# Four attention layers on one core: row-group maxima, value matmuls in two halves of 256 queries, key loads on another queue

## The chip, the cores and the metric

The kernel runs on one core of one Trainium2 chip. The metric is the device time of one execution in microseconds (us). Lower is better.

## What is computed

The program is a stack of four transformer layers on 2048 tokens of width 256. Each layer is `x + cross_attention(layernorm(x), context)` followed by `x + mixture_of_experts(layernorm(x))`. The context has 1601 rows of width 192. Layers 0, 1 and 3 have 16 heads of width 16, layer 2 has 8 heads of width 32. Cut to what the change touches:

```python
q = (x @ Wq + bq).reshape(B, Sq, H, D).transpose(0, 2, 1, 3)      # 2048 queries
k = (y @ wk + bk).reshape(B, -1, H, D).transpose(0, 2, 1, 3)      # 1601 keys
v = (y @ wv + bv).reshape(B, -1, H, D).transpose(0, 2, 1, 3)
attn = jax.nn.softmax(q @ k.swapaxes(-1, -2) / sqrt(D), axis=-1)
x = x + (attn @ v).transpose(0, 2, 1, 3).reshape(B, Sq, E) @ wo + bo
```

## The kernel before

**Tiling.** The queries are cut into 4 blocks of 512, the heads into 4 groups (four heads of width 16, or two of width 32), the keys into 13 tiles of 128 (the last has 65). For each block and each group, 13 steps run over the key tiles. So a layer has 208 steps. The first and the last block are written out, the two in the middle are a hardware loop.

**Precision by stacking.** Queries and keys are split into three bf16 parts each. The tile `k_stack` (`KS`) holds parts of the keys in its partitions, `q_stack` (`QS`) the matching parts of the queries, so that one bf16 matmul over the partitions adds up six products of parts. For heads of width 16 the six products take 96 partitions. Partition 96 holds the mask (or zero) against ones. Partitions 97 to 99 hold ones against the three parts of the negated row maximum. Heads of width 32 need two such stacks (`nsub` is 2), added in the accumulator.

**The work of a step.** `scores` (L1863) multiplies 128 keys by 512 queries, one matmul per head and stack, four in a step. It takes 100 partitions, so the maximum is already subtracted. ScalarE turns each pair of accumulator banks into probabilities (L986). `weigh` (L1877) multiplies the probabilities of the step before by the values `V`: four heads of 32 columns each, one beside the other in the partitions of bank 4, in float32, which makes two passes for each. They are 4 matmuls of 512 queries in the program and 8 in the trace (layer 2: 2 heads of 64 columns, 4 in the trace).

**The side jobs.** The row maxima of a later group are computed ahead, as side jobs that are spread over the steps by `side_schedule` (L66). A "max" job is a matmul of 128 queries by 400 keys over 97 partitions (L1826; two matmuls, over 97 and 96 partitions, in layer 2), into one of three banks in turn, and a maximum over its 400 columns by VectorE (L1257). A bank is reused after VectorE has read it (the wait `sf.at(2)`). Most steps have five such jobs (layer 2: two or three). Other side jobs are "turn" (transposes the maxima, L1829), "den" and "spread" (the denominators, L1832 and L1836), "out" (the output projection, L1848), "turn_x" and "query" (the queries of the next block, L1841 and L1763). In each step two side jobs stand ahead of the scores, the rest between them, and the value matmuls stand at the end. Ahead of the steps, `side_prologue` computes all maxima of group 0 and some of group 1.

**Queues.** SyncE (the queue SP) issues nearly all DMAs in program order: `load_queries` (L474, L480), `store_max_rows` (L489, L494), `store_key_parts` (L437) and `load_keys` (L461). During the experts of layers 0 and 2, `next_keys` stores the key parts of the next layer in eight pieces and, after the fourth and the eighth, waits until they have landed and issues 12 key loads. ScalarE copies each projected piece (L922, L923) into one of two buffers, which come free when their store has landed; GpSimd (POOL) splits it.

Of the kernel before, what the change touches and what calls it, by code (L numbers as in the profile page):

```python
# [6 lines left out]
P = 128  # L7
NT = T // P
Q = 512
# [26 lines left out]

class Count:
# [27 lines left out]

def side_schedule(g, hpg, first, last):  # L66
# [11 lines left out]
    late = [("max", (g + 1) % NG, u, c) for u in range(half, units) for c in range(4)] if nxt1 else []  # L78
    early = [("max", (g + 2) % NG, u, c) for u in range(half) for c in range(4)] if nxt2 else []
# [19 lines left out]
def max_jobs(g, hpg, lo, hi):  # L99
    return [("max", g, u, c) for u in range(lo, hi) for c in range(4)]  # L100
# [35 lines left out]
def build(nc, A, out):  # L136
# [13 lines left out]
    with ctx:  # L150
# [46 lines left out]
        with att:  # L197
# [5 lines left out]
            KS = sb("k_stack", [100, 16, S], bf16, att)  # L203
            V = sb("v", [P, NK, 512], f32, att)
            QS = [sb(f"q_stack{i}", [100, 4, Q], bf16, att) for i in range(4)]
# [9 lines left out]
        with ln2:  # L215
            sb("skip_sums", [P, 4 * 2 * Q + 2 * Q + 16 + Q + NG * Q], f32, ln2)
            sb("skip_keys", [100, 16, S], bf16, ln2)
            sb("skip_values", [P, NK, 512], f32, ln2)
            XN = sb("xn", [P, NT, D], f32, ln2)
# [100 lines left out]
        s_ks = [sem(f"s_ks{g}") for g in range(NG)]  # L320
        s_ql = [sem(f"s_ql{i}") for i in range(4)]
# [59 lines left out]


        @block.sync
        def _(sp):
# [34 lines left out]
            def load_constant_rows(L):  # L419

                ones_flat = const_rows[0:1, 0:S]
                rows = [(96, mask_row if L == 3 else zero_row)]
                if L in (0, 2):
                    rows += [(97, ones_flat), (98, ones_flat), (99, ones_flat)]
                for row, src in rows:
                    sp.dma_start(KS[row:row + 1, :, :], src.unsqueeze(1).to_broadcast([1, 16, S]))\
                      .then_inc(s_ksc, 16)
# [26 lines left out]
            def load_keys(L, g):  # L454

                dh, nsub, hpg = ATT[L]["dh"], ATT[L]["nsub"], ATT[L]["hpg"]
                for row in range(6):
                    part = [0, 1, 2, 0, 1, 0][row]
                    src = k_parts[part].rearrange("(h d) s -> d h s", d=dh)[:, g * hpg:(g + 1) * hpg, :]
                    r, sub = (row, 0) if nsub == 1 else (row % 3, row // 3)  # L460
                    sp.dma_start(KS[r * dh:(r + 1) * dh, 4 * g + sub:4 * g + 4:nsub, :], src)\  # L461
                      .then_inc(s_ks[g], 16)

            def load_queries(L, t, buf):
# [5 lines left out]
                dst = QS[buf]  # L470
                if a["nsub"] == 1:
                    for row, part in enumerate([0, 0, 0, 1, 1, 2]):
                        src = q_parts[part].rearrange("(h d) t -> d h t", d=dh)[:, g * hpg:(g + 1) * hpg, cols]
                        sp.dma_start(dst[row * dh:(row + 1) * dh, :, :], src).then_inc(s_ql[buf], 16)  # L474
                else:
                    for row, part in enumerate([0, 0, 0, 1, 1, 2]):
                        src = q_parts[part].rearrange("(h d) t -> d h t", d=dh)[:, g * hpg:(g + 1) * hpg, cols]
                        r = row % 3
                        sp.dma_start(dst[r * dh:(r + 1) * dh, row // 3::2, :], src).then_inc(s_ql[buf], 16)
                sp.dma_start(dst[96:97, :, :], ones_row).then_inc(s_ql[buf], 16)  # L480

            def store_max_rows(L, g):
# [11 lines left out]
                sp.dma_start(QS[g][96:100, 0:4:a["nsub"], :], src).then_inc(s_mr, 16)  # L494
# [25 lines left out]
            load_keys(0, 0)  # L520
            load_keys(0, 1)

            for L in range(4):
# [8 lines left out]
                if L == 0:  # L532
# [3 lines left out]
                    load_keys(0, 2)  # L536
                    load_keys(0, 3)
# [61 lines left out]
                def next_keys():  # L599

                    if L in (0, 2):
                        load_constant_rows(L + 1)
# [21 lines left out]
                elif L == 1:  # L624
# [39 lines left out]
                    for g in range(NG):  # L664
                        load_keys(2, g)
# [57 lines left out]
        def _(pool):  # L723
# [69 lines left out]
            for L in range(4):  # L793
# [887 lines left out]
        def _(pe):  # L1681
# [4 lines left out]
            ksc, ks, ql, mr = Count(s_ksc), [Count(s) for s in s_ks], [Count(s) for s in s_ql], Count(s_mr)  # L1686
# [65 lines left out]
            for L in range(4):  # L1752
# [21 lines left out]
                ksc.step({0: 4 * 16, 1: 16, 2: 4 * 16, 3: 16}[L])  # L1774
                pe.wait_ge(s_ksc, ksc.at())
                for g in range(NG):
                    ks[g].step(6 * 16)
                for q in range(3):
                    ql[q].step(7 * 16)
                njob, pair, used, turned = [0], [0], [0], [0]  # L1780
                sel = sel16 if dh == 16 else sel32
# [4 lines left out]
                def side(job):  # L1786
# [3 lines left out]
                    if job[0] == "max":  # L1790
                        _, g, u, c = job
                        if u == 0 and c == 0:
                            pe.wait_ge(s_ql[g], ql[g].at())
                            pe.wait_ge(s_ks[g], ks[g].at())
# [470 lines left out]
```

## Time and profile before

| | before |
|---|---|
| median of 3 runs | 4478.63 us (4469.84 to 4485.76) |
| profiled execution | 4481.04 us |
| its span, first to last instruction | 4479.3 us |
| mean granted TensorE clock | 0.926 |
| TensorE matmul busy | 4004.6 us, 89% |
| VectorE busy | 2650.2 us, 59% |
| ScalarE busy | 1937.9 us, 43% |
| GpSimd busy | 322.4 us, 7% |

The page of the profile gives the busy time of each engine over the whole span. The four attention stages lie at about 116 to 775, 1223 to 1885, 2473 to 3104 and 3403 to 4066 us, with the experts between them. PE is TensorE's matmuls, PEld its weight loads. A matmul's duration in the trace has the fill and the drain of the array in it, so the distance from one start to the next is the better measure of what a matmul costs.

### The profile page before, as it was taken

Reading aid. Unit: us, or ns where it says so; the run is one execution under the profiler, and the core shown is the slowest. Engines: PE = TensorE matmul, PEld = TensorE weight load, DVE = VectorE, ACT = ScalarE, POOL = GpSimd, SP = SyncE. Lnnn points to the kernel's source line nnn. Section 1 sums busy time; section 2 is a strip of 40 time slices with the busy share of each in tenths; the row PEclk is TensorE's granted clock in tenths of the full one; section 3 lists DMA queues with packets and bytes.
Section 4 is the critical chain, followed back from the end, with each engine's and each line's share of the span. In section 5 each row is a group of like instructions: output and inputs, shape, how many; then the busy total and the mean of one; then the engine's idle time right before and its main releaser. Section 6 shows DMA issues by size and latency. Waiting matters only on the chain. (4 is left out here: it accounts for less than half of the span.)

```text
span 4479.3 us, 60914 instructions
## 1 busy us (share of the span) xinstructions
PE 4004.6 (89%) x19174; PEld 1813.1 (40%) x19175; DVE 2650.2 (59%) x5801; ACT 1937.9 (43%) x2306; POOL 322.4 (7%) x588
## 2 busy tenths in 40 slices
PE   5999999799899999948993999998889999996894
PEld 2333333566333333335662343443532333333563
DVE  5888785445788888532224555443258887874122
ACT  1567667222166766712331334333103666763110
POOL 2100000200010000040002100000101000000202
PEclk8999999799699999958996999999697999997997
DMA  6000000400000000052104000000400000001145
GB/s 126 25 16 13 13 9 2 82 19 19 24 26 16 10 13 9 1 198 95 32 29 104 26 15 12 12 8 19 66 20 27 20 11 13 10 4 67 61 143 106
DMA packets 131861, 170.58 MB, mean 38 GB/s; under 512 B 30840, under 2 KB 111936, under 8 KB 129539
## 3 DMA queue, kind: packets, MB, share of 16 engines
q1 hardware_dynamic: 121986, 136.07, 11.7%
q0 software_dynamic: 9600, 31.04, 2.4%
q8 instruction: 149, 2.44, 0.2%
q14 instruction: 126, 1.02, 0.1%
HBM read 114.12 MB, written 54.66 MB: 38 GB/s over the span
## 5 line engine op out<-in xcount | busy, mean ns | idle before, releaser
L1257 DVE TENSOR_REDUCE mx<-ps 128x1 f32<-128x400 f32 (+1 forms) x3584 | 1809.0, 565 | 491.1 <-PE ps L1826 482.5
L986 ACT ACTIVATE probs<-ps,zero_col 128x1024 f32<-128x1024 f32 (+1 forms) x1040 | 1113.3, 1111 | 889.5 <-PE ps L1863 889.4
L1826 PE MATMUL ps<-k_stack,q_stack 97*128 97x400 bf16 (+3 forms) x4096 | 1219.5, 347 | 74.5 <-issue 34.8
L1863 PE MATMUL ps<-q_stack,k_stack 100*128 100x512 bf16 (+2 forms) x3328 | 1081.6, 382 | 4.0 <-ACT probs L986 4.0
L1877 PE MATMUL ps<-probs,v 128*32 128x512 f32 (+2 forms) x5824 | 891.9, 607 | 0.2 <-ACT probs L986 0.2
L1826 PEld LDWEIGHTS ps<-k_stack,q_stack 97*128 97x128 bf16 (+1 forms) x4096 | 343.9, 98 | 1173.7 <-DVE mx L1257 712.3
L986 ACT ACTIVATE probs<-ps,mask_col 128x1024 f32<-128x1024 f32 (+1 forms) x416 | 441.0, 1110 | 259.6 <-PE ps L1863 259.6
L1863 PEld LDWEIGHTS ps<-q_stack,k_stack 100*128 100x128 bf16 (+2 forms) x3328 | 324.7, 100 | 315.7 <-ACT probs L986 55.8
L1532 DVE SCALAR_TENSOR_TENSOR x_res<-ps,comb,x_res 128x256 f32<-128x256 f32 x336 | 148.3, 482 | 175.7 <-PE ps L2027 168.6
L1877 PEld LDWEIGHTS ps<-probs,v 128*32 128x32 f32 (+2 forms) x5824 | 140.0, 111 | 228.4 <-issue 220.2
L2027 PE MATMUL ps<-w_down_s,h_t_s 128*128 128x256 f32 x640 | 149.5, 381 | 4.3 <-ACT h_t_s L1088 4.1
L2091 PE MATMUL ps<-w_all,xn_t 128*128 x624 | 144.6, 385 | 3.8 <-ACT xn_t L1056 2.4
L2012 PE MATMUL ps<-xn_t,w_up_s 128*128 128x512 f32 x320 | 147.2, 592 | 0.8 <-issue 0.8
L2070 PE MATMUL ps<-w_all,xn_t 128*128 x312 | 142.7, 600 | 0.4 <-issue 0.4
L2027 PEld LDWEIGHTS ps<-w_down_s,h_t_s 128*128 128x128 f32 x640 | 120.6, 190 | 50.7 <-issue 35.5
L1848 PE MATMUL ps<-wo,o_t 128*128 128x256 f32 x512 | 130.7, 405 | 11.0 <-DVE mx L1257 7.6
L2091 PEld LDWEIGHTS ps<-w_all,xn_t 128*128 128x128 f32 x624 | 118.1, 192 | 43.0 <-issue 28.4
L1056 ACT ACTIVATE xn_t<-ps,tile_bias 128x128 f32<-128x128 f32 x312 | 84.7, 383 | 99.6 <-PE ps L2082 99.4
L1088 ACT ACTIVATE h_t_s<-ps 128x512 f32<-128x512 f32 x80 | 46.7, 596 | 177.0 <-PE ps L2012 176.9
L740 POOL MEMSET wv<- 1x256 f32 x4 | 1.2, 304 | 1670.6 <-DVEq L376 1670.3
L1848 PEld LDWEIGHTS ps<-wo,o_t 128*128 128x128 f32 x512 | 99.3, 200 | 40.7 <-DVE mx L1257 20.5
L2045 PE MATMUL ps<-w_up_s,xn_t 128*128 128x512 f32 x256 | 112.2, 601 | 0.8 <-DVE x_res L1499 0.8
(250 smaller groups left out, 2823.9 us busy)
## 6 DMA issues: line engine op xcount, KB each, us to landing
q_stack<-q_parts SPq DMA_DIRECT2D x384, 64.0 KB, 2.2
k_stack<-k_parts SPq DMA_DIRECT2D x96, 200.1 KB
q_parts<-qk_part SPq DMA_DIRECT2D x32, 384.0 KB, 2.5
w_up<-in_up SPq DMA_DIRECT2D x17, 704.0 KB, 4.3
x_place<-zeros POOLq DMA_DIRECT2D x2, 5120.0 KB, 28.6
k_parts<-qk_part SPq DMA_DIRECT2D x24, 384.0 KB, 3.2
w_all<-in_up SPq DMA_DIRECT2D x5, 1024.0 KB, 21.4
w_all<-in_down SPq DMA_DIRECT2D x5, 1024.0 KB, 23.6
```

The lines of the kernel that those rows point to most:

```text
L986: act.activation(PR[pair[0] % 4][0:r, :, :], PS[0:r, 2 * b:2 * b + 2, :], ACT.Exp, bias=mask_col[0:r, k:k + 1] if L == 3 else zero_col[0:r ...
L1257: ins = dve.reduce_max(MX4[g % 2][:, u, c:c + 1], PS[:, bank, 0:CK[c]], AX.X)
L1532: dve.scalar_tensor_tensor(X[:, t, :], PS[:, b, 0:D], c, X[:, t, :], ALU.mult, ALU.add).then_inc(s_yf, 1)
L1826: last = mm(PS[:, bank, 0:CK[c]], QS[g][0:rows, s, qt * P:(qt + 1) * P], KS[0:rows, ks0, CKO[c]:CKO[c] + CK[c]], start=sub == 0, stop=sub ...
L1848: last = mm(PS[:, bank, 0:D], OT[:, g, i * P:(i + 1) * P], WO[:, g, :], start=g == 0, stop=g == NG - 1)
L1863: last = mm(PS[0:r, b + i, :], KS[0:rows, (g * hpg + jj) * nsub + sub, k * P:k * P + r], QS[g][0:rows, slot_of(jj) + sub, :], start=sub == ...
L1877: last = mm(PS[pw * jj:pw * jj + pw, 4, :], V[0:r, k, (g * hpg + jj) * pw:(g * hpg + jj) * pw + pw], PR[used[0] % 4][0:r, i, :], start=k = ...
L2012: last = mm(PS[0:rows, b, :], up[:, k, off + at:off + at + rows], xnT[:, k, c * Q:(c + 1) * Q], start=k == 0, stop=k == 1)
L2027: last = mm(PS[:, b, 0:D], HTF[(c - 1) % 2][0:rows, t, i * P:(i + 1) * P], WDF[par][0:rows, t, :], start=t == 0, stop=t == len(ft) - 1)
L2045: last = mm(PS[:, t % 8, :], xnT[:, k, t * P:(t + 1) * P], WUS[par][:, k * 512:(k + 1) * 512], start=k == 0, stop=k == 1)
L2070: last = mm(PS[:, half, :], XT1[par][:, k * P:(k + 1) * P], w1.rearrange("p a f -> p (a f)"), start=k == 0, stop=k == 1)
L2091: last = mm(PS[:, 4 + par, 0:D], HB[:, q * P:(q + 1) * P], w2.rearrange("p a f -> p (a f)"), start=q == 0, stop=q == NF // P - 1)
```

## The change

1. **Rows.** For heads of width 16, even heads keep their most significant products (k0q0, k1q0, k0q1) in partitions 0 to 47 and the mask in 48; odd heads keep them in 64 to 111 and the mask in 112, with the other products in the partitions that are left. The odd heads get a seventh product. `scores` then takes 100 partitions for even heads and 116 for odd ones.
2. **Maxima.** A max job takes 49 partitions only (0 to 48, or 64 to 112), and `max_order` lets even and odd heads alternate. In layer 2 it takes the first stack alone: one matmul instead of two.
3. **Value matmuls in halves.** `weigh` runs all heads of queries 0 to 255, then up to two side jobs (`between`), then all heads of queries 256 to 511. `places` sets where side jobs stand: in a step of five, two ahead of the scores, one in their middle, two between the halves.
4. **Loads.** Keys of heads of width 16 take 13 DMAs for a group instead of 6, queries 15 instead of 7, the rows of maxima 2 instead of 1.
5. **Queue.** The key loads for layers 1 and 3 are issued by GpSimd, after all eight pieces are split and their stores have landed, and no longer by SyncE in the middle of the stores.

```diff
+ROWS = ([(0, 0, 0), (16, 1, 0), (32, 0, 1), (52, 2, 0), (68, 1, 1), (84, 0, 2)],
+        [(64, 0, 0), (80, 1, 0), (96, 0, 1), (0, 2, 0), (16, 1, 1), (32, 0, 2), (48, 2, 1)])
+MROW, MAX_ROWS, ALL_ROWS = (48, 112), ((0, 49), (64, 113)), (100, 116)
+def max_order(hpg):
+    if hpg == 2:
+        return [(u, c) for u in range(2 * TPQ) for c in range(4)]
+    return [((2 * j + odd) * TPQ + t, c) for j in range(2) for t in range(TPQ) for c in range(4) for odd in range(2)]
+def places(n, npair):
+    if npair == 1:
+        return [min(n, 1), max(n - 1, 0) // 2, 0, max(n - 1, 0) - max(n - 1, 0) // 2]
+    between, ahead = min(n, 2), min(max(n - 2, 0), 2)
+    rest = n - ahead - between
+    mid = (rest + 2) // 3
+    return [ahead, (rest - mid + 1) // 2, mid, (rest - mid) // 2, 0, between]
@@ next_keys (SyncE)
-                        if L != 1 and u % 4 == 3:
-                            wait_landed(kd)
-                            load_keys(L + 1, u // 2 - 1)
-                            load_keys(L + 1, u // 2)
@@ GpSimd, after split_keys
+                if L in (0, 2):
+                    for c in staged.landed["key"]:
+                        pool.wait_ge(c.sem, c.at())
+                    for g in range(NG):
+                        load_keys(pool, L + 1, g)
@@ side, "max"
-                        for sub in range(nsub):
-                            rows = 97 if sub == 0 else 96
-                            s = slot_of(j) + sub
-                            ks0 = (g * hpg + j) * nsub + sub
-                            last = mm(PS[:, bank, 0:CK[c]], QS[g][0:rows, s, qt * P:(qt + 1) * P],
-                                      KS[0:rows, ks0, CKO[c]:CKO[c] + CK[c]], start=sub == 0, stop=sub == nsub - 1)
+                        lo, hi = MAX_ROWS[j % 2] if nsub == 1 else (0, 97)
+                        last = mm(PS[:, bank, 0:CK[c]], QS[g][lo:hi, slot_of(j), qt * P:(qt + 1) * P],
+                                  KS[lo:hi, (g * hpg + j) * nsub, CKO[c]:CKO[c] + CK[c]], start=True, stop=True)
@@ weigh
+                    for half in range(2):
+                        cols = slice(half * Q // 2, (half + 1) * Q // 2)
+                        for j in range(npair):
...
+                                last = mm(PS[pw * jj:pw * jj + pw, 4, cols],
+                                          V[0:r, k, (g * hpg + jj) * pw:(g * hpg + jj) * pw + pw],
+                                          PR[(used[0] + j) % 4][0:r, i, cols], start=k == 0 and half == 0, stop=k == NK - 1,
...
+                        if half == 0:
+                            for job in between:
+                                side(job)
```

## Rows read from the trace of the kernel before

**Rows 1.** The page, busy time: engine, us (share), instructions.

```profile
PE 4004.6 (89%) x19174; PEld 1813.1 (40%) x19175; DVE 2650.2 (59%) x5801; ACT 1937.9 (43%) x2306; POOL 322.4 (7%) x588
```

**Rows 2.** Busy time by stretch: stretch, length, busy of each engine, clock, DMA share, GB/s.

```profile
116.00:775.00 659.00, 646.78 (x3754) 229.08 (x3753) 521.69 (x1103) 454.10 (x445) 21.18 (x24) 1.00 0.04 13
2473.00:3104.00 631.00, 629.11 (x2928) 248.90 (x2926) 306.02 (x632) 245.69 (x237) 21.17 (x24) 1.00 0.04 13
1850.00:1884.00 34.00, 32.81 (x197) 7.46 (x194) 5.56 (x16) 31.78 (x32) 0.00 (x0) 1.00 0.01 1
2452.00:2471.00 19.00, 16.57 (x71) 4.11 (x69) 18.39 (x42) 0.00 (x0) 0.00 (x0) 1.00 0.14 41
```

**Rows 3.** Timeline of PE, layer 0: start us, us, work, count.

```profile
402.05 1.07 PE L1877 MATMUL ps<-probs,v 128*32 128x512 f32 x8
403.05 0.52 PE L1826 MATMUL ps<-k_stack,q_stack 97*128 97x401 bf16 x2
403.41 0.59 PE L1863 MATMUL ps<-q_stack,k_stack 100*128 100x512 bf16 x2
403.84 0.33 PE L1826 MATMUL ps<-k_stack,q_stack 97*128 97x400 bf16 x1
404.01 0.38 PE L1863 MATMUL ps<-q_stack,k_stack 100*128 100x512 bf16 x1
...
404.62 0.33 PE L1826 MATMUL ps<-k_stack,q_stack 97*128 97x401 bf16 x1
404.89 1.06 PE L1877 MATMUL ps<-probs,v 128*32 128x512 f32 x8
```

**Rows 4.** The same at the end of layer 1, steps without side jobs.

```profile
1849.95 1.04 PE L1863 MATMUL ps<-q_stack,k_stack 100*128 100x512 bf16 x4
1850.92 1.06 PE L1877 MATMUL ps<-probs,v 128*32 128x512 f32 x8
1851.91 0.60 PE L1863 MATMUL ps<-q_stack,k_stack 100*128 100x512 bf16 x2
```

**Rows 5.** Timeline of PE, experts of layer 3: transposes of 128 and 64 partitions.

```profile
4255.45 0.38 PE L2153 MATMUL ps<-ident,x_expert 128*128 128x128 f32 x2
4255.77 0.27 PE L2153 MATMUL ps<-ident,x_expert 64*128 64x64 f32 x1
4255.97 0.44 PE L2153 MATMUL ps<-ident,x_expert 128*128 128x128 f32 x2
```

**Rows 6.** Timeline of DVE, the maxima of one step of layer 0.

```profile
403.43 2.50 DVE L1257 TENSOR_REDUCE mx<-ps 128x1 f32<-128x401 f32 x5
```

**Rows 7.** Timeline of PE, layer 2, one step with three max jobs.

```profile
2906.87 1.08 PE L1877 MATMUL ps<-probs,v 128*64 128x512 f32 x4
2907.88 0.86 PE L1826 MATMUL ps<-k_stack,q_stack 97*128 97x401 bf16 x4
2908.58 1.03 PE L1863 MATMUL ps<-q_stack,k_stack 100*128 100x512 bf16 x4
2909.55 1.08 PE L1877 MATMUL ps<-probs,v 128*64 128x512 f32 x4
```

**Rows 8.** Timelines of SP and PE, the start of layer 1's maxima.

```profile
1172.42 2.69 SPq L474 DMA_DIRECT2D q_stack<-q_parts  x6
1175.16 0.53 SPq L480 DMA_DIRECT2D q_stack<-const_rows  x1
1177.29 3.22 PE L1826 MATMUL ps<-k_stack,q_stack 97*128 97x401 bf16 x7 [8.33 <-issue]
```

**Rows 9.** Timelines of SP, ACT, DVE, PE and landing of stores, experts of layer 0.

```profile
835.86 7.03 SPq L461 DMA_DIRECT2D k_stack<-k_parts  x12
859.78 0.60 ACT L922 ACTIVATE qk<-ps 128x512 f32<-128x512 f32 x1 [22.23 <-DMA k_parts<-qk_part]
848.04 0.42 DVE L1431 TENSOR_TENSOR comb<-prob_s,r_s 128x256 f32<-128x256 f32 x1
869.66 0.69 PE L2012 MATMUL ps<-xn_t,w_up_s 128*128 128x512 f32 x1 [0.82 <-issue]
DMA to landing us min/median/max: 16.7/17.0/17.2
```

**Rows 10.** Timeline of ACT, experts of layer 2, the same wait.

```profile
3196.15 0.60 ACT L922 ACTIVATE qk<-ps 128x512 f32<-128x512 f32 x1 [19.80 <-DMA k_parts<-qk_part]
```

**Rows 11.** GpSimd's DMA issues of L853, ns min/median/max.

```profile
L853 POOL DMA_DIRECT2D w_all<-in_up x3: 543/561/592, 2027.0 to 2029.2; - x3
```

More of the change, by code:

```diff
@@ L77, in side_schedule @@
     half = units * 3 // 8
-    late = [("max", (g + 1) % NG, u, c) for u in range(half, units) for c in range(4)] if nxt1 else []
-    early = [("max", (g + 2) % NG, u, c) for u in range(half) for c in range(4)] if nxt2 else []
+    late = max_jobs((g + 1) % NG, hpg, half, units) if nxt1 else []
+    early = max_jobs((g + 2) % NG, hpg, 0, half) if nxt2 else []
     jobs = late + early[:6] + ([("turn", (g + 1) % NG)] if nxt1 else []) + early[6:]
@@ L320, in build @@
         s_ks = [sem(f"s_ks{g}") for g in range(NG)]
+        s_kt = [sem(f"s_kt{g}") for g in range(NG)]
         s_ql = [sem(f"s_ql{i}") for i in range(4)]
@@ L380, in key_rows, with load_keys @@
             return P if k < NK - 1 else KREM
+        def load_keys(eng, L, g):
+            dh, nsub, hpg = ATT[L]["dh"], ATT[L]["nsub"], ATT[L]["hpg"]
+            done = s_kt[g] if L in (1, 3) else s_ks[g]
+            heads = k_parts.rearrange("r (h d) s -> r d h s", d=dh)[:, :, g * hpg:(g + 1) * hpg, :]
+            if nsub == 1:
+                for odd in range(2):
+                    for row, part, _ in ROWS[odd]:
+                        eng.dma_start(KS[row:row + dh, 4 * g + odd:4 * g + 4:2, :], heads[part][:, odd::2, :])\
+                           .then_inc(done, 16)
+            else:
+                for i, (_, part, _) in enumerate(ROWS[0]):
+                    sub, r = i // 3, i % 3 * dh
+                    eng.dma_start(KS[r:r + dh, 4 * g + sub:4 * g + 4:2, :], heads[part]).then_inc(done, 16)
         @block.sync
@@ L421, in load_constant_rows @@
                 ones_flat = const_rows[0:1, 0:S]
[L422 to L427, printed above, removed]
+                rows = [mask_row if L == 3 else zero_row] + [ones_flat] * 3
+                for i, src in enumerate(rows):
+                    if ATT[L]["nsub"] == 1:
+                        for odd in range(2):
+                            sp.dma_start(KS[MROW[odd] + i:MROW[odd] + i + 1, odd::2, :],
+                                         src.unsqueeze(1).to_broadcast([1, 8, S])).then_inc(s_ksc, 16)
+                    else:
+                        sp.dma_start(KS[96 + i:97 + i, 0::2, :], src.unsqueeze(1).to_broadcast([1, 8, S]))\
+                          .then_inc(s_ksc, 16)
             def store_key_parts(u):
@@ L493, in store_max_rows @@
                 src = m_parts[:, 0:units * P].rearrange("r (j x) -> r j x", x=Q)
-                sp.dma_start(QS[g][96:100, 0:4:a["nsub"], :], src).then_inc(s_mr, 16)
+                if a["nsub"] == 1:
+                    for odd in range(2):
+                        sp.dma_start(QS[g][MROW[odd]:MROW[odd] + 4, odd::2, :], src[:, odd::2, :]).then_inc(s_mr, 16)
+                else:
+                    sp.dma_start(QS[g][96:100, 0::2, :], src).then_inc(s_mr, 16)
             x_chunks = A["x"].rearrange("(c t p) d -> c p t d", t=TPQ, p=P)
@@ L1918, in iteration @@
                                     pe.wait_ge(s_os, cs.at())
-                                weigh(g, k - 1)
+                                weigh(g, k - 1, jobs)
+                            else:
+                                for job in jobs:
+                                    side(job)
                 njobs = sum(len(s) for g in range(NG) for s in side_schedule(g, hpg, False, False))
```

110 lines of the change are left out of this document (54 added, 56 removed).

## The prediction

> **What bounds the kernel now.** I read the busy times first [rows 1]: PE is busy 89% of the span. Then I read the stretches of the attention stages [rows 2]: in layer 0 PE is busy 647 of 659 us at full clock, VectorE 522, ScalarE 454. So attention, some 2614 of the 4479 us, is paced by PE in program order, with VectorE next. Then I read one step [rows 3]. From value block to value block it lasts 404.89 - 402.05 = 2.83 us, and PE never pauses: a max matmul starts its successor 0.17 us later (403.84 to 404.01), a scores matmul 0.215 us later (403.41 plus two of them is 403.84). Five maxima and four scores are 0.86 + 0.86 = 1.72 us. That leaves 1.11 us for the value block. A matmul's duration has some 0.17 us of fill and drain in it (a scores matmul lasts 0.38 and is followed after 0.215), so of the block's 1.07 us it streams 0.90, with a seam of 0.05 between its two passes: 0.85 us of columns. So about 0.25 us of each step is neither.
>
> Where these 0.25 us lie is the key to the change. The last max starts at 404.62 and is through at 404.79, yet the values start at 404.89: 0.10 us. The values end their streaming near 402.95, yet the next max starts at 403.05: 0.10 us. The other 0.05 us goes to the seam between the two passes. Steps without side jobs show the same [rows 4]: the scores start at 1849.95, four of them are through at 1850.81, the values start at 1850.92. The array pauses about 0.10 us whenever the shape of the tile changes, from 128 columns to 32 and back. A change in the number of rows costs the same: a transpose of 128 partitions is followed after 0.11 us by its like (the pair at 4255.45 lasts 0.38 us, one of them 0.27), but the one of 64 partitions starts only at 4255.77, 0.21 us after the second, and the next one of 128 partitions again 0.20 us later, though the 64 columns between them need half as long [rows 5]. I price one switch at 0.10 us, bounds 0.09 and 0.15.
>
> **The change, part by part.**
>
> *Layers 0, 1, 3: switches.* A step of five now has two switches. New order: two maxima (49 partitions), two scores, one max, two scores, first value half, two maxima, second value half. That is a switch in front of each of these seven blocks: five more, +0.50 us. A step with "den", "spread", "out" or "query" as its sixth job has ten, eight more. Walked through all 208 steps by the diff's placing, a layer gets 1095 more switches: +110 us (bounds 99 and 164).
>
> The Trainium skill says the same in TensorEngine Tiling (Array Packing), Key Properties: changing the tiling mode, not merely the tile, drains the engine. By that rule, too, five more pauses stand in a step; the trace agrees with it at 0.10 us each.
>
> *Pairs.* Two neighbouring maxima now lie in partitions 0 to 48 and 64 to 112 and go to different banks. The value matmuls show that tiles side by side in columns run together (four heads in one block of 1.07 us [rows 3], where one after the other would be four times as long). For tiles side by side in rows the trace has nothing. Bounds: the second max is free (saves 0.17 us) or costs its full 0.17 us. I take nearly free, saving 0.16, since the column case is the nearest row. A layer has 320 such pairs: -51 us.
>
> The same skill, TensorE: Matmul & The Clock Gate, Part 3, states that matmuls in distinct row groups overlap, with 3.07 times the speed for four; no run here shows it yet.
>
> *Halves.* The second half repeats the seam between passes and loads the values' weights again: 0.04 us in 207 value blocks, +8 us.
>
> *VectorE's chain.* It takes 0.48 us a maximum (five in 2.50 us, the last one 0.56) and starts 0.38 us after the matmul (403.05 to 403.43) [rows 3, 6]. With three banks, the second max ahead of the scores needs the bank of the first max between the halves: 0.38 + 0.56 + about 0.05 us after that one's start, 0.99 us. PE is there after 0.18 (pair) + 0.10 + 0.47 (half) + 0.10 = 0.85 us. So a new wait of 0.13 us stands in each of 123 steps of five, +16 us, with the scores queued behind it. Against it go waits of PE on VectorE that exist now around "out", "den" and "query" jobs, 659 - 647 = 12 us in a layer [rows 2], most of which slower steps cover: -12.
>
> Sum of a layer: 110 - 51 + 8 + 16 - 12 = +71 us (a step of five: 2.83 + 0.50 - 0.32 + 0.04 + 0.13 = 3.18). Three layers: **+213 us**.
>
> *Layer 2.* A step of two max jobs lasts 2909.55 - 2906.87 = 2.68 us, with four max matmuls from 2907.88 to 2908.58 [rows 7]; one of three jobs is two matmuls longer, 3.02. One matmul a job goes, 0.17 us each; the maxima keep 97 partitions, so they switch only around the value halves: +0.20 and +0.04. Three jobs: -0.52 + 0.24 = -0.28; two: -0.34 + 0.24 = -0.10. Over the layer's steps 468 jobs save 80 us, 382 more switches and 207 seams add 38 + 8: **-34 us** (bounds -38 and -14, by the price of a switch). VectorE is busy 306 of 631 us [rows 2] and does not take over.
>
> *Query and maxima loads.* SP needs 2.69 us for six issues, 0.45 each [rows 8]. The first maxima wait for the first buffer: eight issues more, 3.6 us, in each of layers 0, 1 and 3. In layer 0 the key loads and two further buffers stand in the same queue ahead of the rows of maxima, with 14 more issues a pair of groups; PE is at most some 10 us later there. Inside the steps a group lasts some 40 us and hides 7 us of issues; if that cover were gone each group would start up to 4 us late. Together **+18 us** (bounds 8 and 30).
>
> *Key loads.* Today the stores of pieces five and six stand behind 12 key loads and land after 17.0 us; ScalarE waits 22.23 us for the buffer (there is nothing else to put it to), and with it the values' projections, which PE needs before its experts at 869.66 [rows 9]. Without the loads ahead, such stores land in about 3 us. So 14 us come back in layer 0; VectorE's routing is done at 848.5 [rows 9], PE would start near 855, so it is late next and doesn't bind. In layer 2 the wait is 19.80 us [rows 10], some 13 us come back. **-27 us** (bounds -34 and 0). GpSimd's 52 loads, at its 0.56 us an issue [rows 11], are 29 us, and it is idle for 280 us of experts in layer 0 and 130 in layer 2: hidden.
>
> **The sum.** +213 - 34 + 18 - 27 = +170 us on the profiled 4481.0, 4651. The median of the runs shown lies 2.4 us lower: 4649, in round numbers 4650 us, 3.8% slower.
>
> **The rivals.**
>
> *Row switches are free* (chance 0.12). If going between 49 and 97 or more partitions costs nothing, and only value blocks pause, 709 of the 1095 switches of a layer go, -71 us. VectorE's chain gives part back: a step of five would be 2.68 + 0.04 + 0.13 = 2.85 us, no better than now. So a layer is at +12 us at most, at 0 if the chain runs smoother: 0 to 36 for three, with - 34 + 18 - 27 that is 4436 to 4472: not slower. It decides from a row switch under about 0.03 us. Rows 5 speak against it.
>
> *Pairs don't overlap* (0.10). Then 51 us a layer stay and the wait of 16 goes: +35 each, 4755. Against it: the value block.
>
> *49 partitions are not treated as a smaller tile* (0.08). Then the change does not do what it says: maxima run one after the other, but without row switches. A layer has 390 more switches around and between the halves: 39 + 8 - 12 = +35; total 3 x 35 - 43 = +62, 4541. Against it: the transposes of 64 partitions.
>
> *Density* (0.07). A step of five gets 50 matmuls and weight loads for 34. If the clock drops for a tenth of the steps, 2.2 us of streaming double there: 0.1 x 624 x 2.2 = 137 us, 4787; a PE that can't be fed so densely would look similar. Against a drop: at the end of layer 1, 16 steps (32 activations) take 34 us and stream 1.71 of 2.13 us each, 80%; in layer 2's prologue 71 matmuls of 0.17 us stream 12 of 19 us, 63%. Both kept clock 1.00 [rows 2]; the new step streams 2.2 of 3.18 us, 70%.
>
> **How the numbers follow.** The forecast case holds 0.63 and spans 4590 to 4710 (switch price, loads). The range takes in the second rival and the third, 4515 to 4760, 0.8 of the chance; free row switches and a drop of density stay outside. Within 0.3% (what can be told from no change here) is 4465 to 4492. Faster: 0.07, from free row switches. Same: 0.04. Slower: 0.89.
>
> **What would show it.** In the profile after: pairs of L1826 that start within 0.02 us of each other; 0.10 us between a pair's end and the next scores; steps of five near 3.18 us; in layer 2 steps of three near 2.75 us; the ACT wait on the key stores near 3 us instead of 22; PE's first expert matmul of layer 0 some 15 us sooner after the end of attention. I would be wrong if the gap at a change from 49 to 100 partitions were much smaller than 0.10 us in bf16, if the pairs were serial, or if VectorE's chain held PE longer than 0.13 us a step.

## The result, and the profile after the change

The changed kernel takes 4680.3 us (median of 4 runs, 4670.6 to 4685.0), the one before 4474.3 us (median of 4, 4469.8 to 4485.8). The ratio is 1.046, with a 95% interval of 1.044 to 1.048. The forecast was 4650 us in a range of 4515 to 4760, slower with a chance of 0.89.

| | before | after |
|---|---|---|
| profiled span | 4479.3 us | 4675.1 us |
| mean granted clock | 0.926 | 0.915 |
| first scores of layer 0 | 116.2 us | 145.0 us |
| scores stage, layer 0 | 658.8 us | 728.0 us |
| layer 1 | 661.2 us | 734.7 us |
| layer 2 | 630.7 us | 610.7 us |
| layer 3 | 663.0 us | 740.0 us |
| step of five max jobs (median start to start) | 2.83 us | 3.205 us |

The page of the changed kernel first, busy times of its engines (engine, us, share):

```profile
PE 4244.2 (91%) x24486; PEld 1833.5 (39%) x24487; DVE 2684.1 (57%) x5801; ACT 1943.1 (42%) x2306; POOL 374.2 (8%) x692
```

PE issues 5312 matmuls more than in [rows 1] (5824 more in the value blocks, which are cut in two, 512 fewer maxima in layer 2) and stays the engine that paces. The four attention stages, read by stretch (stretch, length, busy PE, PEld, DVE, ACT, POOL, clock, DMA share, GB/s), against [rows 2]:

```profile
145.00:873.00 728.00, 720.93 (x5402) 235.79 (x5401) 527.95 (x1103) 454.75 (x445) 21.21 (x24) 0.99 0.05 12
1315.00:2050.00 735.00, 728.24 (x5402) 236.92 (x5403) 528.94 (x1104) 455.07 (x444) 21.21 (x24) 0.98 0.05 12
2637.00:3247.00 610.00, 608.29 (x3284) 243.52 (x3283) 319.77 (x634) 247.26 (x237) 21.20 (x24) 0.98 0.04 13
3535.00:4275.00 740.00, 732.87 (x5401) 236.96 (x5399) 528.73 (x1104) 454.99 (x444) 21.20 (x24) 0.97 0.05 12
```

VectorE's and ScalarE's times in layer 0 are those of before within 1.3%. PE's work was rearranged, and the stage is 69 us longer. One step of layer 0, the timeline of PE (start us, us, work, count), which answers [rows 3]:

```profile
402.55 0.64 PE L1922 MATMUL ps<-probs,v 128*32 128x256 f32 x8
403.12 0.51 PE L1868 MATMUL ps<-k_stack,q_stack 49*128 49x400 bf16 x2
403.56 0.61 PE L1905 MATMUL ps<-q_stack,k_stack 100*128 100x512 bf16 x2
404.10 0.34 PE L1868 MATMUL ps<-k_stack,q_stack 49*128 49x400 bf16 x1
404.37 0.61 PE L1905 MATMUL ps<-q_stack,k_stack 100*128 100x512 bf16 x2
404.91 0.64 PE L1922 MATMUL ps<-probs,v 128*32 128x256 f32 x8
405.48 0.34 PE L1868 MATMUL ps<-k_stack,q_stack 49*128 49x400 bf16 x2
405.76 0.62 PE L1922 MATMUL ps<-probs,v 128*32 128x256 f32 x5
```

Read the starts. The single max of 404.10 is followed by scores at 404.37, after 0.27 us; before it was 0.17 [rows 3]. Two scores from 403.56 would be through at 403.99, and the max starts at 404.10. Each change of shape costs 0.10 us, also between 49 and 100 partitions. The pair at 405.48 lasts 0.34 us in all, as long as one: its two matmuls start at 405.483 and 405.486. The pair at 403.12 lasts 0.51 us: the second starts 0.165 us after the first, when VectorE has freed its bank. VectorE's line for the step, against [rows 6]:

```profile
402.65 2.50 DVE L1298 TENSOR_REDUCE mx<-ps 128x1 f32<-128x400 f32 x5 [0.66 <-PE ps L1868]
```

It takes the same 2.50 us for five maxima, and it had waited 0.66 us for PE before them.

A step of three jobs in layer 2, against [rows 7]:

```profile
2905.59 0.65 PE L1922 MATMUL ps<-probs,v 128*64 128x256 f32 x4
2906.17 0.34 PE L1868 MATMUL ps<-k_stack,q_stack 97*128 97x401 bf16 x1
2906.44 0.65 PE L1922 MATMUL ps<-probs,v 128*64 128x256 f32 x4
2907.03 0.34 PE L1868 MATMUL ps<-k_stack,q_stack 97*128 97x400 bf16 x1
2907.21 0.60 PE L1905 MATMUL ps<-q_stack,k_stack 100*65 100x512 bf16 x2
2907.65 0.33 PE L1868 MATMUL ps<-k_stack,q_stack 97*128 97x400 bf16 x1
2907.82 0.60 PE L1905 MATMUL ps<-q_stack,k_stack 100*65 100x512 bf16 x2
2908.35 0.65 PE L1922 MATMUL ps<-probs,v 128*64 128x256 f32 x4
```

It lasts 2908.35 - 2905.59 = 2.76 us. The maxima of 97 partitions sit beside the scores without a pause (2907.03 to 2907.21, 0.18), and pay 0.10 us only at the value halves.

### The profile page after: what moved, and what is told of

The parts are those of the page before. It is cut to its first block and busy times, and to the rows that moved or that the text cites. A ratio compares the mean times of both kernels' runs of the same rounds, so it can differ in the third digit from the quotient of the medians.

```text
span 4675.1 us, 72302 instructions
## 1 busy us (share of the span) xinstructions
PE 4244.2 (91%) x24486; PEld 1833.5 (39%) x24487; DVE 2684.1 (57%) x5801; ACT 1943.1 (42%) x2306; POOL 374.2 (8%) x692
## 5 line engine op out<-in xcount | busy, mean ns | idle before, releaser
L1298 DVE TENSOR_REDUCE mx<-ps 128x1 f32<-128x400 f32 (+1 forms) x3584 | 1840.3, 567 | 668.2 <-PE ps L1868 660.2
L1868 PE MATMUL ps<-k_stack,q_stack 49*128 49x400 bf16 (+3 forms) x3584 | 1002.4, 359 | 77.7 <-issue 41.5
L1922 PE MATMUL ps<-probs,v 128*32 128x256 f32 (+2 forms) x11648 | 1071.7, 397 | 1.1 <-ACT probs L1027 1.1
L1905 PE MATMUL ps<-q_stack,k_stack 100*128 100x512 bf16 (+4 forms) x3328 | 1029.3, 390 | 6.1 <-ACT probs L1027 6.1
L1868 PEld LDWEIGHTS ps<-k_stack,q_stack 49*128 49x128 bf16 (+1 forms) x3584 | 281.6, 94 | 1109.6 <-DVE mx L1298 603.7
L1922 PEld LDWEIGHTS ps<-probs,v 128*32 128x32 f32 (+2 forms) x11648 | 287.1, 112 | 507.2 <-issue 483.8
L1905 PEld LDWEIGHTS ps<-q_stack,k_stack 100*128 100x128 bf16 (+4 forms) x3328 | 246.5, 100 | 344.7 <-issue 244.6
```

Of the source, the lines that this page charges most:

```text
L1298: ins = dve.reduce_max(MX4[g % 2][:, u, c:c + 1], PS[:, bank, 0:CK[c]], AX.X)
L1868: last = mm(PS[:, bank, 0:CK[c]], QS[g][lo:hi, slot_of(j), qt * P:(qt + 1) * P], KS[lo:hi, (g * hpg + j) * nsub, CKO[c]:CKO[c] + CK[c]], s ...
L1905: last = mm(PS[0:r, b + i, :], KS[0:rows, (g * hpg + jj) * nsub + sub, k * P:k * P + r], QS[g][0:rows, slot_of(jj) + sub, :], start=sub == ...
L1922: last = mm(PS[pw * jj:pw * jj + pw, 4, cols], V[0:r, k, (g * hpg + jj) * pw:(g * hpg + jj) * pw + pw], PR[(used[0] + j) % 4][0:r, i, cols ...
```

## The experiments

All edits start from the kernel before or from the changed one, as said. Ratios are to the kernel before, on the same chip, with 95% intervals. "Step of five" is the median distance between the first value matmuls of steps with five max jobs.

**1. The halves alone.** The kernel before with the value blocks in halves and the new places; its maxima keep 97 partitions.

```diff
+                    for half in range(2):
+                        cols = slice(half * Q // 2, (half + 1) * Q // 2)
...
+                        if half == 0:
+                            for job in between:
+                                side(job)
```

> The kernel before with the value matmuls in halves and the new places of the side jobs alone; maxima keep 97 partitions, loads and queues stay. Theory (a change of tile shape costs 0.10 us, either in rows or columns): only the halves add switches, two in a step, +0.20 +0.04, so a step of five side jobs goes from 2.83 to about 3.07 us, layers 0, 1 and 3 grow by 30 to 45 us each (to 690 to 705), layer 2 by 45 (to 676), in all 4610 to 4650 us. Rival (the halves themselves, their reloads and the dense stream of instructions cost the time, and the rows of the maxima cost nothing): a step of five is at 3.2 us or more here too, as it is in the changed kernel with its 3.205. Start of layer 0's steps: if its delay of 29 us in the changed kernel comes from the clock under 49-partition maxima, it is back at about 116 us here.

4617.1 us, ratio 1.034 (1.031 to 1.037). Step of five 3.073 us, layers 0, 1 and 3 at 692.8, 692.7 and 693.9 us. That is two switches and a seam on 2.83 us: 0.20 + 0.04. So the halves by themselves cost 3.4%. This isn't a share of the 4.6%, for experiment 3 has no halves and loses 3.9%. Splitting a block that is alone in its shape adds two switches when a job of another shape stands in the cut.

**2. Neighbouring maxima in the same 64 partitions.** The changed kernel with another order, so that no two neighbours lie in different row groups.

```diff
-    return [((2 * j + odd) * TPQ + t, c) for j in range(2) for t in range(TPQ) for c in range(4) for odd in range(2)]
+    return [(u, c) for u in range(4 * TPQ) for c in range(4)]
```

> The changed kernel, but neighbouring max jobs belong to the same head, so both lie in the same 64 partitions and can't run side by side. Theory (pairs in different partitions really overlap, 0.16 us each): the pair between the value halves takes 0.33 instead of 0.17 us, while the pair ahead of the scores is already 0.165 us apart for VectorE's bank; a step of five goes from 3.205 to about 3.37 us, a layer by +25 to +35 us, all three +75 to +105, total 4755 to 4785. Rival (the overlap is only in the records, the array shares its time): no change beyond 0.3%, 4680.

4806.6 us, ratio 1.076 (1.065 to 1.087), step of five 3.379 us, 0.174 more than with the pairs. Timeline of PE, layer 0:

```profile
404.27 0.64 PE L1922 MATMUL ps<-probs,v 128*32 128x256 f32 x8
404.84 0.51 PE L1868 MATMUL ps<-k_stack,q_stack 49*128 49x401 bf16 x2
405.29 0.64 PE L1922 MATMUL ps<-probs,v 128*32 128x256 f32 x8
```

The two maxima between the halves take 0.51 us instead of 0.34. Of the two pairs of a step, 0.16 each, one is given back as the wait for VectorE's bank. So the rival "pairs don't overlap" is out: the pairs work, but they earn less than the row switches that they need. The total lies above the 4755 to 4785 us that were expected, and the clock has part in it: in the middle of layers 0, 1 and 3 it stood at half for 48, 31 and 44 us, in the changed kernel for 7, 24 and 17.

**3. Whole value blocks, maxima at their old places.**

```diff
-                    for half in range(2):
-                        cols = slice(half * Q // 2, (half + 1) * Q // 2)
+                    for j in range(npair):
```

> The changed kernel with its value matmuls whole and the side jobs placed as in the kernel before (two ahead, the rest one by one between the scores); rows, maxima and loads as changed. Theory (0.10 us for each change between 49 and 100 or 116 partitions): a step of five has eight switches, six more than before, and one pair, so about 3.26 us although no value matmul is split; layers 0, 1, 3 at 730 to 745 us; layer 2, with one matmul a job and no halves, at about 553 us, a three-job step at 2.50; total 4610 to 4640. Rival (halves are the cost): a step of five at or under 2.83 us, layers at 660 or less, total near 4400.

4640.1 us, ratio 1.039 (1.036 to 1.042), step of five 3.276 us, though no value block is split. The old places put maxima between the scores one by one, which makes six row switches: 2.83 + 6 x 0.10 - 0.16 for the one pair = 3.27.

**4. Whole value blocks, maxima in two clusters.** Two ahead of the scores, the rest together behind them.

```diff
                                     scores(g, k, j, i)
-                                    for job in slot[cut[2 * j + i]:cut[2 * j + i + 1]]:
-                                        side(job)
+                            for job in slot[2:]:
+                                side(job)
```

> The changed kernel with whole value matmuls and the side jobs in two groups, two ahead of the scores and all others behind them, ahead of the values. Theory: a step of five has four switches (into and out of the values, out of and into the maxima), two more than before, and two pairs side by side: 1.965 + 3 x 0.172 + 0.20 + some 0.05 of waiting for VectorE = 2.74 us against 2.83 before; layers 0, 1, 3 at 660 to 668, layer 2 at 553, total 4400 to 4440, under the kernel before by 1 to 2 percent. Rival (VectorE is the bound once maxima come in threes): steps of five at 2.9 us or more, total over 4470.

4455.0 us, ratio 0.9965 (0.9951 to 0.998), above the 4400 to 4440 us that was expected. The step came out: 2.759 us.

```profile
402.29 0.34 PE L1868 MATMUL ps<-k_stack,q_stack 49*128 49x400 bf16 x2
402.57 1.04 PE L1905 MATMUL ps<-q_stack,k_stack 100*128 100x512 bf16 x4
403.55 0.58 PE L1868 MATMUL ps<-k_stack,q_stack 49*128 49x400 bf16 x3
404.05 1.06 PE L1919 MATMUL ps<-probs,v 128*32 128x512 f32 x8
```

Two added switches (+0.20) against 0.27 that pairs save. Yet layer 0 takes 681.4 us, 23 more than before. One reason is the other steps: with all jobs in one cluster PE waits for VectorE's banks, as its list of waits in layer 0 says (who, for what: us, times, longest).

```profile
PE ps L1890 <- DVE mx L1298: 6.8, 12, 0.9
PE ps L1874 <- DVE mx L1298: 6.1, 13, 0.5
PE ps L1878 <- DVE mx L1298: 6.0, 13, 0.5
```

Before, the waits for VectorE in layer 0 were 6.6 us in all. The 43 steps with five max jobs and "den", "spread" or "out" take 0.29 us more each, 12 us. The larger reason is the clock: in layer 0 it stands at half for 39.0 us in all, in seven stretches, and for 3.7 us before. At half of each stretch that is some 18 us (an estimate), while the 123 steps of five give back 9. The gain of the total is layer 2's (552.3 us).

**5. A shorter VectorE chain.** The changed kernel with each maximum over half of its columns; the other half of the maxima's keys is left out.

```diff
-dve.reduce_max(MX4[g % 2][:, u, c:c + 1], PS[:, bank, 0:CK[c]], AX.X)
+dve.reduce_max(MX4[g % 2][:, u, c:c + 1], PS[:, bank, 0:CK[c] // 2], AX.X)
```

> The changed kernel, but VectorE takes each maximum over 200 of the 400 columns (it leaves out half of each row of scores in the maxima, so the subtracted value is not always the largest). Theory (VectorE's turn on the three banks holds the second max ahead of the scores 0.165 us behind the first in every step of five): the reduction falls from 0.56 to about 0.35 us, the two maxima ahead start within 0.01 us, a step of five goes from 3.205 to 3.04 us, a layer by 20 to 22 us, total 4610 to 4625. Rival (the second max waits for the array, not for its bank): no change of the 0.165 us, total 4680.

4576.2 us, ratio 1.020 (1.017 to 1.023). The step of five is 3.043 us, as expected, 0.16 less than 3.205. So VectorE holds PE 0.16 us in a step of five and no more: with maxima of 0.37 us instead of 0.57 the kernel is still 2.0% slower than before. The total is lower than expected because the maxima ahead of the steps also became shorter, by 14 us in layers 1 and 3, 8 in layer 2 and 7 in layer 0, which the expectation had missed.

**6. More loads.** The kernel before with the keys' and queries' loads cut by even and odd heads, 12 and 13 DMAs a group for 6 and 7.

```diff
-                        sp.dma_start(dst[row * dh:(row + 1) * dh, :, :], src).then_inc(s_ql[buf], 16)
+                        for odd in range(2):
+                            sp.dma_start(dst[row * dh:(row + 1) * dh, odd::2, :], src[:, odd::2, :]).then_inc(s_ql[buf], 16)
```

> The kernel before with its key and query loads of layers 0, 1 and 3 cut by odd and even heads: 24 instead of 12 key loads for two groups, 13 instead of 7 query loads, the same bytes; maxima with 97 partitions as before. It asks why the steps of layer 0 begin at 145 us in the changed kernel and at 116 before. Theory (under 49-partition maxima the granted clock of the prologue stays at the lower level, so its projections take twice as long): the loads alone cost 4 to 8 us, scores begin at 120 to 124 us. Rival (the longer queue of SyncE delays the rows of maxima): scores begin at 140 us or later. Layers 1 and 3: first maxima 2.7 us later. Total +10 to +16 us, or +35 by the rival.

4491.8 us, ratio 1.001 (1.000 to 1.003), 6 us more where 10 to 16 were expected; first scores at 123.2 us. The loads cost 2 to 7 us of the 29 at the start: with the loads of before the first scores come at 116.2 us in the kernel before and at 119.0 to 120.9 in experiments 1, 7, 8 and 9.

**7. The queue of the key loads.** The kernel before; GpSimd issues the key loads of layers 1 and 3 behind its splits.

```diff
-                        if L != 1 and u % 4 == 3:
-                            wait_landed(kd)
-                            load_keys(L + 1, u // 2 - 1)
-                            load_keys(L + 1, u // 2)
+                    for g in range(NG):
+                        load_keys(pool, L + 1, g)
```

> The kernel before with part 5 of the change alone: the 24 key loads of layers 1 and 3 are issued by GpSimd after all stores have landed. Theory (the stores of pieces five and six no longer queue behind the loads): ScalarE's wait of 22 us in the experts of layer 0 falls to 3 to 5, PE begins those experts 14 to 17 us sooner, in layer 2 13 to 15 us, total -27 to -32 us, 4436 to 4441 against 4467. Rival (the loads now compete with the experts' weights and give it back): PE waits for weights in the experts of layer 0, the gain under 15 us.

4457.9 us, ratio 0.993 (0.991 to 0.995). From the last scores to the first expert matmul it is 77.8 us in layer 0 (94.7 before) and 102.2 in layer 2 (118). Part of it is lost again: the experts of layer 0 take 11 us more. PE waits 9.07 us there for weights, which SyncE loads beside the keys. PE's timeline, and from the list of DMAs GpSimd's loads (count, KB each, median us to landing):

```profile
897.72 2.07 PE L2017 MATMUL ps<-xn_t,w_up_s 128*128 128x512 f32 x2 [9.07 <-DMA w_down_s<-in_down]
...
k_stack<-k_parts POOLq DMA_DIRECT2D x24, 200.1 KB, 16.2
```

**8. One maximum matmul in layer 2.** The kernel before; in layer 2 the products of the second stack are left out of the maxima, as in the changed kernel.

```diff
-                        for sub in range(nsub):
+                        last = mm(PS[:, bank, 0:CK[c]], QS[g][0:97, slot_of(j), qt * P:(qt + 1) * P],
```

> The kernel before with one matmul instead of two in each max job of layer 2 (97 partitions, the products of the first stack; the maximum is then of slightly coarser scores, which softmax allows), values whole, places as before. Theory: PE is the bound of layer 2, so each job gives 0.17 us: steps of three jobs 3.02 to 2.50 us, of two 2.68 to 2.33, 468 jobs 80 us, layer 2 from 631 to about 552 us, total 4386 to 4390 against 4467. Rival (VectorE or ScalarE takes over): steps of three stay over 2.7 us, the gain under 50 us.

4406.3 us, ratio 0.982 (0.980 to 0.984). Layer 2 takes 551.9 us. In the changed kernel it takes 610.7: 59 of the 79 us that this part alone earns are given back. Some 50 of them are the halves', the rest is a stretch of 20.5 us at half clock.

**9. The two good parts together.** Experiments 7 and 8 in one kernel.

> The kernel before with two parts of the change alone, each measured by itself already: GpSimd issues the key loads of layers 1 and 3 after all stores have landed (0.993 of before), and layer 2's maxima take one matmul over the first stack instead of two (0.982; as in the changed kernel, the products of the second stack are left out of the maxima). Rows, order and places of layers 0, 1 and 3 stay as before, so no switch of tile shape is added. My theory: the two parts act in different stages and add up, 0.993 x 0.982 = 0.975 of before, about 4370 us, between 4360 and 4390; layer 2's attention stage 552 us, last scores to first expert matmul 78 us in layer 0 and 102 in layer 2, the experts of layer 0 about 289 us. Rival: the sooner start of the experts is worth something only when layer 2 ends as before; now that layer 2's steps are paced more tightly, the two overlap in what they save, and the sum is near that of the larger part alone, 4400 us or more.

4369.8 us, ratio 0.978 (0.976 to 0.980), so it beats both kernels, by 2.2% and, from the two ratios, 6.5%. Layer 2 takes 551.7 us, layers 0, 1 and 3 are as before (663.6, 658.7, 659.1). The product of the two ratios is 0.975, or 0.971 to 0.980 with the ends of their intervals, so the parts add up within what can be told.

**10 and 11. 64 and 65 partitions.** Experiment 6 had left over 20 us at layer 0's start without a shown cause, and no kernel so far had changed the row count alone. Two kernels do: the kernel before with 64 or 65 partitions in the maxima of layers 0, 1 and 3.

```diff
-                            rows = 97 if sub == 0 else 96
+                            rows = 64 if nsub == 1 else 97 if sub == 0 else 96
```

> The kernel before, with one edit: in layers 0, 1 and 3 the max matmuls take 64 partitions instead of 97 (what is left out of the maxima: the small products in partitions 64 to 96 and the mask, which is all ones here). Layout, loads, queues, order, places and instruction counts are those of before. My theory: the price is that of the shape alone, 0.10 us in front of each change between 64 and 100 or more partitions. A step of five gets four or five more of them, so 3.27 us instead of 2.83 (3.28 was measured with 49 partitions and the changed loads), each of the three layers 730 to 740 us, total 4690 to 4720. And the late start of layer 0's scores is the clock's doing, from the fewer rows of the prologue's maxima: first scores near 140 us as in the changed kernel, with TensorE at half clock through 69 to 106 us. Rival for the start: it comes from the changed layout or its loads; then the first scores stay at 116 to 120 us and the clock is full from 69 us on as before. Rival for the step: the pauses come with the two places 0 and 64 of the tile and not with its size; then the step stays at 2.83 us and the time at before's.

> The same edit with one partition more: 65 instead of 64. My theory: the array goes by tile sizes, and 65 partitions are the same mode as 100, so no switch is added: step of five 2.83 us, layers 657 to 665 us, total within 0.3% of before (4465 to 4490). The clock of the prologue tells rows from mode: if the granted clock goes by how many partitions work, 65 is as 64 and the first scores come at 130 us or later; if it goes with the mode, they come at 116 to 122 us. I have no row that decides between these two; I take the second at 0.6. Rival for the step: each change of the number of partitions costs a pause; then the step is 3.27 us and the total 4690 to 4720 as with 64.

With 64: 4852.4 us, ratio 1.084 (1.081 to 1.088), step of five 3.442 us. With 65: 4513.9 us, ratio 1.008 (1.005 to 1.011), step of five 2.830 us. Timelines of PE, layer 0, first 64, then 65:

```profile
403.47 0.39 PE L1863 MATMUL ps<-q_stack,k_stack 100*128 100x512 bf16 x1
403.79 0.34 PE L1826 MATMUL ps<-k_stack,q_stack 64*128 64x401 bf16 x1
404.06 0.39 PE L1863 MATMUL ps<-q_stack,k_stack 100*128 100x512 bf16 x1
```

```profile
403.44 0.34 PE L1826 MATMUL ps<-k_stack,q_stack 65*128 65x400 bf16 x1
403.62 0.38 PE L1863 MATMUL ps<-q_stack,k_stack 100*128 100x512 bf16 x1
403.84 0.33 PE L1826 MATMUL ps<-k_stack,q_stack 65*128 65x401 bf16 x1
404.01 0.38 PE L1863 MATMUL ps<-q_stack,k_stack 100*128 100x512 bf16 x1
```

From scores to max to scores: 0.32 and 0.27 us with 64, 0.22 and 0.17 with 65. One partition decides over 0.10 us at each change. A second place of the tile isn't needed for it, since both kernels lie at partition 0. My count for 64 was wrong, and with it the expected 4690 to 4720 us: I had taken the step of experiment 3, which has a pair in it. Six added switches without a pair are 2.83 + 0.61 = 3.44. With 65 the total, too, missed its 4465 to 4490 us. The steps are those of before; what is longer is the start of layer 0 and, in layers 1 and 3, stretches at half clock of 20.5 and 13.7 us (3.4 and 6.8 before).

The Trainium skill, TensorEngine Tiling (Array Packing), Tiling Modes, lists 64-row tiles as a mode of their own beside 128 rows; the border between 64 and 65 agrees with it.

The start of layer 0 came out the other way than I had thought likelier. The scores start at 142.0 us with 64 partitions and at 137.5 with 65, so it isn't the mode. The stretch 69 to 106 us in four kernels (columns as above). The kernel before:

```profile
69.00:106.00 37.00, 31.41 (x133) 16.52 (x131) 33.78 (x71) 10.06 (x23) 9.56 (x12) 1.00 0.62 107
```

The changed kernel:

```profile
69.00:106.00 37.00, 33.87 (x73) 12.35 (x72) 18.30 (x37) 5.52 (x13) 9.60 (x12) 0.50 0.30 82
```

With 64 partitions:

```profile
69.00:106.00 37.00, 36.97 (x76) 13.91 (x75) 18.26 (x37) 5.90 (x14) 9.60 (x12) 0.50 0.32 69
```

With 65 partitions:

```profile
69.00:106.00 37.00, 36.97 (x82) 17.73 (x82) 20.77 (x42) 5.91 (x14) 9.61 (x12) 0.50 0.38 86
```

With 97 partitions the engine ran at 2.4 GHz here and did 133 matmuls; with 49, 64 or 65 it stayed at 1.2 GHz, though it was as busy, and did 73 to 82. All six kernels with 97 partitions reach 2.4 GHz within this stretch (granted clock 0.84 to 1.00), none of the seven with fewer does (0.50). From the first maximum to the first scores it is 51.6 to 55.0 us with 97 partitions, 70.3 with 65 and 77.2 with 64. The scores of layer 0 start at 116.2 us (before), 120.0 (experiment 1), 123.2 (6), 119.0 (7), 120.9 (8) and 119.2 (9) with 97 partitions, and at 137.5 to 146.4 with 49 to 65. Fewer partitions at work brought the higher clock later.

## Why the prediction was right, point by point

| term | predicted | measured |
|---|---|---|
| a switch | 0.10 us | 0.10 us, by rows too (1, 3, 10) |
| two pairs in a step of five | -0.32 us | -0.174, net of the wait in the next row (2); starts 3 ns apart |
| VectorE's wait in it | +0.13 us | +0.16 us (5) |
| halves in a step of five | +0.24 us (two switches, seam) | +0.243 us (1) |
| step of five | 3.18 us | 3.205 us |
| layers 0, 1, 3 | +213 us | +219.7 us |
| layer 2 | -34 us | -20.0 us |
| loads, with the start of layer 0 | +18 us, at most 10 of it at that start | +28.8 us at that start, +7.1 at layers 1 and 3 |
| experts sooner | -27 us | -31.5 us, and +7.2 back |
| not in the sum | 0 | -15.5 us |
| sum | +170 us | +195.8 us |

**Switches, pairs, halves.** These held, and with them the side of the forecast. The three stages gained 69.2, 73.5 and 77.0 us for 71 each. In that lies some clock, a term that the sum had at nothing: at half clock the stages spent 3.7, 9.3 and 11.1 us before and 11.5, 28.9 and 38.0 after. If a stretch at half clock costs half its length, 4, 10 and 13 us are the clock's (an estimate). Without them each layer gained some 64 us, and my 71 was 7 us too high; that the three add up to 219.7 for 213 is luck. The stretches lie at the start of a stage and behind the gap of up to 3 us at the hardware loop's edge. One in the changed kernel, by stretch (clock is the third number from the end):

```profile
1693.00:1716.00 23.00, 22.83 (x104) 5.88 (x108) 10.16 (x20) 10.03 (x10) 0.00 (x0) 0.50 0.09 21
1717.00:1730.00 13.00, 13.00 (x89) 4.84 (x88) 9.25 (x18) 6.36 (x6) 0.00 (x0) 1.00 0.00 1
```

The kernel before had 3.4 us at half clock at this edge of layer 1. Over all kernels such a stretch is 0 to 10 us long in layers 0, 1 and 3 with 97 partitions, and mostly 7 to 48 with 49, 64 or 65 (none in layer 0 with 65). So the fewer rows have part in it. They aren't all of it: in layer 2, whose maxima keep 97 partitions, the changed kernel has one of 20.5 us and the kernel before none. The rival "density" had the right object, the clock, and the wrong place: in the changed kernel the steady steps of the three layers hold the higher clock but for one stretch of 3.4 us in layer 3.

**Layer 2.** Its steps came out (2.763 and 2.590 us for 2.74 and 2.58). Of the missing 14 us a stretch of 20.5 us at half clock is 10, and the steps' 0.01 to 0.02 us are 2.

**The start of layer 0** is the step that failed, the term "PE is at most some 10 us later there". It priced issues on SP (2 to 7 us, experiment 6) and left out the clock of the prologue, which accounts for the rest: experiments 10 and 11, with the loads of before, start 17 to 26 us later than the five kernels with 97 partitions and these loads. [Rows 2] showed full clock only for stretches with 97 partitions or more, and I took it as given for 49.

**Key loads.** ScalarE's waits for the stores fell from 29.7 to 9.5 us in layer 0, their longest from 22.23 [rows 9] to 3.15 us, and in layer 2 from 27.7 to 8.9, the longest from 19.80 [rows 10] to 4.55. ScalarE's timeline after:

```profile
929.93 0.23 ACT L963 ACTIVATE qk<-ps 128x65 f32<-128x65 f32 x1 [3.15 <-DMA k_parts<-qk_part]
3324.49 0.60 ACT L963 ACTIVATE qk<-ps 128x512 f32<-128x512 f32 x1 [4.55 <-DMA k_parts<-qk_part]
```

From last values to first expert matmul it is 17 us less in layer 0 and 14.5 in layer 2, for 14 and 13. But "hidden" was said of GpSimd's issues, which are, and not of the transfers. These meet the experts' weights: after the change a load of `w_down_s` takes 12.5 to 18.1 us to land, where its median before was 2.1, and PE waits for it once (timelines of POOL and PE):

```profile
949.58 26.05 POOL L414 DMA_DIRECT2D k_stack<-k_parts  x52 [3.50 <-DMA k_parts<-qk_part]
...
984.72 6.01 PE L2063 MATMUL ps<-xn_t,w_up_s 128*128 128x512 f32 x8 [5.11 <-DMA w_down_s<-in_down]
```

SyncE issued this load at 966.5 us. The queues show two phases (queue: packets, MB, share of 16 engines). From 966 to 974 us no packet of SyncE's queue moved:

```profile
q0 software_dynamic: 346, 1.11, 102.8%
```

From 975 to 979 us both queues did:

```profile
q0 software_dynamic: 141, 0.43, 79.8%
q1 hardware_dynamic: 147, 0.14, 24.9%
```

The Trainium skill, DMA: Bandwidth & Descriptors, Queues, rings and completion order, says that an engine takes one packet from each queue in turn. The second phase agrees: 147 packets for 141, and since SyncE's are of 1.0 KB and GpSimd's of 3.0, a quarter of the bytes. The first phase doesn't come out of it, and its 8 us are nearly half of the 18.1 to landing; experiment 7 has the same, 9 us without a packet of SyncE's. Its cause stays open.

**The rest.** Layers 1 and 3 start 3.5 us later behind the experts each. The last stretch, after the attention of layer 3, became 14 us shorter, nearly all of it in the shared expert (53.8 for 68.4 us). In the kernel before PE sat idle in it seven times, for nothing that the profile shows, and the clock fell; after the change there is no such wait. From PE's waits of the kernel before, 4171 to 4197 us:

```profile
PE ps L2012 <- issue: 9.5, 7, 2.1
```

This isn't the change's doing. The shared expert takes 52.7 to 54.1 us in experiments 1 to 4 and 9 and 67.7 to 68.5 in experiments 5 to 8, 10 and 11, and experiment 5 is the changed kernel but for the width of VectorE's maxima. Its cause stays open. Such 14 us are 0.3% of the time, as much as experiment 4 gained.

**The rivals.** Free row switches: out by experiments 3 and 10. Pairs in series: out by experiment 2. 49 partitions no smaller tile: out by experiments 10 and 11. The sum missed by 26 us: 7 in the three layers, 14 in layer 2, 18 in the loads and the start of layer 0, 3 in the key loads with what they delay, less 15 that were not in it. These 15 are luck: without them the two profiles would lie some 210 us apart, for 170 forecast.

## What to carry to other kernels

Count the changes of tile shape in a step before you move a matmul: each costs about 0.10 us here, nearly half of a scores matmul's 0.215, and 49 or 64 partitions are another shape than 65 to 116. Row-group pairs earn 0.16 us each, so they pay only if the matmuls of one shape stand together, and then the next limit is how many banks the reading engine has left free. Take a change apart before you keep or drop it: two parts of it alone made the kernel 2.2% faster, while the whole was 4.6% slower.

## What the runs showed of the hardware

- The border of the row mode lies between 64 and 65 partitions: scores start 0.27 us after a max of 64 partitions and 0.17 us after one of 65. Both lie at partition 0, so the size alone is enough for the pause.
- Two bf16 matmuls in partitions 0 to 48 and 64 to 112 with different banks start 3 ns apart.
- The granted clock of a stretch went with the rows at work: in the same prologue it was 0.50 for 37 us at 92 to 100% busy with 49 to 65 partitions, and 1.00 at 85% busy with 97. The border between 64 and 65 has no visible part in it, for 65 partitions start the scores 21 us after the 116.2 of before, and 64 start them 26 us after it.
- Loads on GpSimd's queue delay those on SyncE's, from 2.1 to 12.5 and 18.1 us for 128 KB. For 8 us nothing moved on SyncE's queue, then the packets of the two went one for one (147 and 141 in 4 us).
